# Half the per-partition scratch for GpSimd's DMA descriptors (16384 to 8192 bytes) in a four-layer graph network on one core

## What is computed

```python
edge_index = jnp.stack([src, dst])
x = _layernorm(x + _L0_gnn_ref(x, edge_index, edge_attr_96, ...))   # attention: exp(clip(sum K[src]*Q[dst]*E)), weighted V[src] summed per dst
x = _layernorm(x + _L1_gnn_ref(x, edge_index, ...))                 # mean and max over neighbours, two batch norms, leaky relu
x = _layernorm(x + _L2_gnn_ref(x, weight, bias, src, dst))          # degree-scaled sum over neighbours, then a matmul
x = _layernorm(x + _L3_gnn_ref(x, edge_index, edge_weight, ...))    # edge-weighted sum of (x @ W)[src], layer norm
```

## Time and profile before

| | |
|---|---|
| three timed runs | 5175.81, 5184.86, 5187.15 us |
| median | 5184.86 us |
| span of the profiled execution | 5246.3 us (the profile lists no separate device time for it) |
| POOL busy | 3200.4 us, 61% of the span |
| PE busy | 2714.9 us, 52% |
| DVE busy | 1982.1 us, 38% |
| ACT busy | 1353.8 us, 26% |
| gathers in POOL's queue | 832 in each pass, 3328 in all |
| packets of GpSimd's descriptors (q0) | 133120 packets, 245.58 MB |

### The profile page before, as it was taken

One profiled execution on the slowest core, in us unless ns is written; L12 is line 12 of the kernel. 1 busy time (PEld: TensorE's weight loads), 2 busy tenths in 40 slices (PEclk: granted clock), 3 DMA queues, 4 the chain that ended last, 5 costly groups with the idle time before them and its releaser, 6 DMA issues.

```text
span 5246.3 us, 56090 instructions
## 1 busy us (share of the span) xinstructions
PE 2714.9 (52%) x15042; PEld 2473.5 (47%) x15042; DVE 1982.1 (38%) x4498; ACT 1353.8 (26%) x4318; POOL 3200.4 (61%) x3366
## 2 busy tenths in 40 slices
PE   6666676666756666566683543332334333333334
PEld 6666676666645555556552432222224222222234
DVE  3555545555655555555554111111113221122124
ACT  1121112222333333333343321211112121111113
POOL 4555555556356666666646666666665666666664
PEclk7676666767777777777785555555555555555555
DMA  7655555555433333333321111111112111111111
GB/s 193 156 142 140 148 137 139 149 143 144 125 94 85 81 84 83 82 83 83 83 60 42 35 35 35 35 35 35 35 35 46 35 36 34 35 35 34 35 35 44
DMA packets 337349, 409.90 MB, mean 78 GB/s; under 512 B 212224, under 2 KB 248691, under 8 KB 336957
## 3 DMA queue, kind: packets, MB, share of 16 engines
q0 software_dynamic: 133120, 245.58, 19.7%
q1 hardware_dynamic: 203933, 160.75, 11.7%
HBM read 386.26 MB, written 19.77 MB: 77 GB/s over the span
## 4 chain that ended last, share of the span: by engine, by line
another core or an unknown queue 32%; PE 19%; DVE 15%; POOL 14%; issue 14%; ACT 3%; DMA 1%; SPq 1%; ACTq 0%; DVEq 0%; POOLq 0%
POOL rows L563 14%; PE bank L655 10%; DVE same L1557 3%; DVE first_only L1256 2%; PE bank L669 2%; DVE first_only L1395 2%; DVE same L1256 2%; PE bank L668 1%; DVE prod L1325 1%; DVE score L1327 1%; DVE prod L1323 1%; PE bank L752 1%; DVE first_only L1264 1%; PE bank L759 1%
## 5 line engine op out<-in xcount | busy, mean ns | idle before, releaser
L655 PE MATMUL bank<-same,rows 128*96 128x128 f32 x4992 | 1059.8, 385 | 1468.8 <-issue 540.6
L655 PEld LDWEIGHTS bank<-same,rows 128*96 128x96 f32 x4992 | 917.5, 246 | 1593.7 <-issue 866.8
L563 POOL DMA_INDIRECT rows<-kv_table,src_idx x832 | 789.7, 949 | 610.0 <-DVE msg L1335 357.0
L563 POOL DMA_INDIRECT rows<-pair_table,src_idx x832 | 786.4, 945 | 520.5 <-issue 208.6
L563 POOL DMA_INDIRECT rows<-h_table,src_idx x832 | 788.7, 948 | 426.9 <-issue 235.0
L938 ACT COPY acc<-bank 96x511 f32 (+1 forms) x832 | 479.4, 576 | 2205.1 <-remote 1582.2
L563 POOL DMA_INDIRECT rows<-ci_table,src_idx x832 | 785.0, 943 | 412.6 <-issue 239.1
L1256 DVE TENSOR_TENSOR same<-bank,rank_col 128x512 f32<-128x512 f32 x624 | 420.6, 677 | 1000.7 <-remote 587.9
L1557 DVE TENSOR_SCALAR same<-iota_s,rank_col,src_hi 128x128 f32<-128x128 f32 x832 | 235.0, 359 | 906.7 <-remote 748.2
L655 PE MATMUL bank<-same,msg 128*105 128x128 f32 x1664 | 366.3, 391 | 384.5 <-ACT acc L940 362.7
L655 PEld LDWEIGHTS bank<-same,msg 128*105 128x105 f32 x1664 | 321.8, 268 | 398.2 <-DVE same L1256 200.9
(11 more groups left out here) (168 smaller groups left out, 2899.5 us busy)
## 6 DMA issues: line engine op xcount, KB each, us to landing
first_only<-in_attr_cols SPq DMA_DIRECT2D x104, 384.0 KB
first_only<-q_table SPq DMA_DIRECT2D x832, 48.0 KB
first_only<-rank_rows SPq DMA_DIRECT2D x104, 256.0 KB
first_only<-keep_rows SPq DMA_DIRECT2D x104, 192.0 KB
rows<-kv_table,src_idx POOLq DMA_INDIRECT x832
rows<-pair_table,src_idx POOLq DMA_INDIRECT x832
rows<-ci_table,src_idx POOLq DMA_INDIRECT x832
rows<-h_table,src_idx POOLq DMA_INDIRECT x832
```

The costliest lines, as they stand in the source:

```text
L563: pool.indirect_dma_start(rows[:, k, j, 0:width], None, table, bass.IndirectOffsetOnAxis(ap=src_idx[:, t:t + 1], axis=0)).then_inc(rows_in ...
L655: mm = pe.matmul(out[0:nrow, here], left(j), right(j), start=(j == 0), stop=(j == TQ - 1), skip_group_check=True)
```

## The change

The reserved piece of each partition is half as long: 8192 bytes in place of 16384. Everything allotted after it starts 8192 bytes lower in each partition. No instruction is added, removed or moved on any engine (PE, DVE, ACT, POOL and SP have the same rows in the same order), and no tile, loop or wait of the kernel changes.

```diff
-    nc = _bacc.Bacc("TRN2", target_bir_lowering=False, num_devices=1)
+    nc = _bacc.Bacc("TRN2", target_bir_lowering=False, num_devices=1, dynamic_dma_scratch_size=8192)
```

## The result

The changed kernel takes 5215.3 us (median of 5 runs, 5210.51 to 5230.11) against 5187.15 us (5 runs, 5175.81 to 5199.14): ratio 1.0058, 95% interval 1.0036 to 1.0079, or +28 us. The forecast was 5187 us with a range to 5204.

The account below looks back on a forecast made before the run. No engine was taken as full over the span, POOL busiest at 61% and PE at 52%. Recycling at +2 us and addresses at nothing, added to the median of 5184.9 us, gave 5187 us, range 5170 to 5204.

Parts of the forecast that it names:

- What bounds the kernel: Whole kernel: no engine full, POOL busiest at 61%; DVE and PE hold POOL back in pass one, third pass most sensitive.
- The mark of 0.55 us is the recycling: Before some gathers: gaps of 0.55 us, not 0.30, every 104 gathers mark recycling of a descriptor ring.
- Half the scratch halves the period: POOL's gathers: recycling every 52 gathers in place of 104, 63 events in place of 31, 32 more.
- The price of an event is 0.25 us at most: POOL's gathers: a visible recycling costs 0.55 - 0.30 = 0.25 us; in steady running it is hidden.
- the sum's upper end: All passes: all 32 new recyclings visible and on the path, 32 x 0.25 = 8.0 us.
- the choice of 1.6 us: POOL, all passes: 12 of 31 visible gives 3.1 us; half kept, 1.6 us, taken as +2 us.
- The halving for the first two passes: Passes one and two: POOL's waits for DVE and mostly PE cover added recycling, so half of 3.1 us is kept.
- Cheaper when it gives back fewer: Recycling: if price follows the gathers recycled, twice as many events at half the price add 0 us.
- Addresses at nothing: All tiles: standing 8192 bytes lower costs nothing, bounded by the timed runs' spread of 0.2%.
- Slow rival, recycling waits for rows under way: Last three passes: each recycling waits for a landing, 67 us more, 5252 us, extreme 5385; chance 0.11.
- Fast rival, the unnamed waits: Last two passes: POOL's 4.5 us stops depend on the scratch; up to 298 us gained, 4887 us; chance 0.02.
- Busy times, grid, gaps: Profile after: 1.25 us per gather, POOL busy 3200 us, last passes 1189 us, 0.55 us gaps every 52 or 47 gathers.

Follow-up runs that it names:

- e4: Scratch of 4096 bytes, a quarter, against the unchanged kernel: ratio 1.0065 (1.0031 to 1.0098).
- e7: Scratch of 16192 bytes, 192 less than full, against the unchanged kernel: ratio 1.0044 (1.0029 to 1.0058).
- e8: Scratch of 12288 bytes, three quarters, against the unchanged kernel: ratio 0.9996 (0.9985 to 1.0007).
- e3: Scratch of 8256 bytes, 64 more than half, against the unchanged kernel: ratio 0.9986 (0.9962 to 1.0009).
- e1: The unchanged kernel run again, scratch 16384 bytes, no edit: ratio 0.9985 (0.9962 to 1.0007).
- e2: Scratch of 8192 bytes plus an unused 8192-byte tile keeping all other tiles at their old addresses, against the unchanged kernel: ratio 1.0049 (1.0024 to 1.0074).
- e12: The changed kernel run again, scratch 8192 bytes and four buffers, against the unchanged kernel: ratio 1.0049 (1.0024 to 1.0074).
- e11: Scratch of 2048 bytes, an eighth, against the unchanged kernel: ratio 0.9997 (0.9969 to 1.0024).

## Why it is slower

**The size sets the place.** Collected, with k from 0:

| scratch, bytes | recyclings at | in its quad | ratio |
|---|---|---|---|
| 16384 | 113 + 104k | second | 0.9985; with one more gather 1.0006 |
| 16192 | 112 + 100k | first | 1.0044 |
| 12288 | 85 + 76k | second | 0.9996 |
| 8256 | 57 + 48k (not seen) | second | 0.9986 |
| 8192 | 56 + 44k | first | 1.0058, 1.0049; tiles in place 1.0049; one more gather 1.0068 |
| 4096 | 28 + 16k | first | 1.0065 |
| 2048 | 14 + 4k | third | 0.9997 |
| 8192, six buffers | 56 + 36k, in the second pass 868 + 36k | first | 1.0152 |
| 8256, six buffers | not seen | | 1.0071 |

With four buffers one rule gives all the periods: when the scratch is full, GpSimd gives back whole quads, and at least nine gathers stay behind. 113 - 9 = 104; 56 - 9 = 47, and the last whole quad before that is 44. Periods are then multiples of four, so all recyclings of a size fall on the same place in the quad. With six buffers 56 - 36 = 20 stay, so nine is no constant of the chip. A rule that fits both is that the last quads begun stay, one fewer than there are buffers: three with four buffers, five with six. That is a fit. What makes a quad the unit (it shares one semaphore here) and why the number of buffers counts was not tried. The periods 104, 100, 44, 36 and 16 are read from many places of their traces; 76 and 4 rest on one place each, and 48 on the rule alone. All five programs with recyclings on a quad's first gather and four buffers lose 0.4 to 0.7%. The four with them elsewhere take the time of the kernel before, within their intervals, and that kernel is such a one itself.

**The price follows the gathers given back, and the wait uncovers it.** In the second pass a first-gather recycling adds about 0.45 us for 16 gathers, 0.75 for 44 and 1.4 for 100: roughly 0.25 + 0.012 us for each. The six-buffer form, which took no part in this fit, gives 2.79 - 2.1 = 0.7 for 36, where the fit says 0.68. This is why 207, 75 and 33 of them cost nearly alike (e4, the change, e7): the gathers given back are about 3328 in every case. Were every event visible, the fit would give 92, 59 and 48 us; measured are 34, 28 and 23, and the intervals are too wide to test the steps between them.

On a second gather behind one that waited, the same work (by the fit 1.5 us for 104 gathers) shows only 0.25, since 1.25, one gather's slot of the earlier trace rows, hides it. At 76 or 48 gathers (about 1.2 and 0.8 us) it shows nothing, as in e8 and e3. Behind a gather that had not waited it shows nothing either, even at 104: in the trace of e1 all 20 such places have the usual 0.30, and all 11 behind a wait have 0.54 or 0.55. My reading is that GpSimd prepares gathers ahead of the one being made, and that a first gather after a wait has nothing made ahead. The numbers fit this; no run looks inside GpSimd.

**Where the 28 us are.** Three traces with half the scratch (after, e2, e12; the first is not of a group) against three of the other form (e1, e3, e11), means from one pass's first gather to the next's (the last to the end of the span): first pass 1427.8 against 1403.7 (+24), second 1334.6 against 1326.0 (+9), third 1208.8 against 1207.2 (+2), fourth 1215.4 against 1212.6 (+3). Together that is more than 28, since the traced runs are not the median ones. In the second pass 19 x 0.75 = 14 us of longer waits give 9. In the last two, where POOL rarely waits at such a place (6 and 5 of 19), they give little. In the first pass 18 recyclings of 0.75 us are 13.5 us at most, while the loss is about 24, though the three traces without the loss differ by 25 us among themselves (1395.0, 1396.1, 1419.9; the last is e3, whose traced run is the slowest of its twelve). So the 24 us are uncertain, and whether a delay of POOL grows in the first pass is not settled.

## The prediction, step by step

- **What bounds the kernel.** Right in kind: in the second pass a delay of POOL does lengthen the pass. Wrong in place: I named the third and fourth passes as the sensitive ones, by the share of POOL's line in the chain, and the first as covered by its waits for DVE. The loss lies the other way round, in the second pass for certain and in the first by the means above. A wait for a free buffer is not slack: POOL's next gathers start late by what is added behind it.
- **The mark of 0.55 us is the recycling.** Right, and so is the first lap of 113 or 56 gathers.
- **Half the scratch halves the period.** Nearly: 44 and not 52 or 47, since twelve gathers stay behind. The numbers 63 or 70 became 75, so 44 events more and not 32.
- **The price of an event is 0.25 us at most.** This is the step that failed. I took the visible price from rows in which every event stood on a quad's second gather, half hidden by the first, and carried it over to a kernel in which the events could stand elsewhere. "A gather right behind one that had waited" was the clue, and I read it as when the event shows and not as how much of it. Behind a wait for a buffer, on a first gather, an event adds about 0.75 us for 44 gathers, three times that price. With it the sum's upper end of 32 x 0.25 = 8.0 us was too low, and the choice of 1.6 us stands against a measured 28. The halving for the first two passes, as covered by the waits for DVE and PE, failed with it: the second pass alone is 9 us longer.
- **Cheaper when it gives back fewer.** I had this as a reason for 0. The price does fall, from about 1.4 us at 100 gathers to 0.45 at 16, but a fixed part of some 0.25 us stays, and it evens out only if the place stays the same.
- **Addresses at nothing.** Right (e2).
- **Slow rival, recycling waits for rows under way.** Not the cause (e11 holds two gathers fewer than can be outstanding and loses nothing). It seems to exist all the same, once, at the start of the second pass. In e8 the pass's first rows were in use at 1495.06, 13.0 us after the last gather of their quad had started, and POOL went on 1.3 us later, about the price of a recycling of 76; in e11 it went on 0.5 us after the same event. That it waited for this landing is my reading. It added 1.76 and 0.08 us.
- **Fast rival, the unnamed waits.** Wrong: within a group the last two passes differ by 10 us or less over all sizes of the scratch with four buffers.
- **Busy times, grid, gaps.** I expected 0.95 us and 1.25 us a gather in steady running, POOL at 3200: all so. The last two passes, expected within 3 us of 1189, took 1183.8 and 1183.5 from their first gather to the end of their last. That is the difference between groups and not the change, for the unchanged kernel of e1 has 1181.1 and 1182.6. I expected gaps of 0.55 us on a finer grid: there are none.

## What to carry to other kernels

When a periodic piece of work shows in a trace, ask at which place of the loop it falls and what hides it there, before its price is carried over: here 64 bytes more scratch moved it by one gather and took away the loss of 0.5 to 0.6%, while an eighth of the scratch cost nothing. If several gathers share a buffer and a semaphore, choose the scratch so that recycling does not fall on the gather that waits for the buffer, and count the places again when the number of buffers changes. And a wait for a free buffer on the engine that feeds the others is not spare time for work behind the wait.

## What the runs showed of the hardware

- GpSimd's recycling of descriptor space costs about 0.25 us plus 0.012 us for every gather of 128 rows given back (from 0.45, 0.75 and 1.4 us at 16, 44 and 100 gathers). It gives back whole quads here. With four buffers it keeps nine to twelve gathers, with six and 8192 bytes it keeps twenty.
- 2048 bytes of scratch per partition, room for 14 gathers, are as good as 16384 for this kernel (0.9997, 0.9969 to 1.0024).
- The same kernel differs by 1.2% from one group of runs to another (5186.9 and 5249.3 us).
